# DRAM scratch of the split queries and keys with a gap behind every two heads, and each store issued in two

## What is computed

```python
h = tok(x)                 # embedding (8000 x 128) + positions, 4 layers: 8-head attention, norm, 512-wide ReLU MLP, norm
h = h + nystrom(norm(h))   # landmark attention with a pseudo-inverse and a convolution
h = h + moe(norm(h))       # frequency transform, 8 experts, 2 taken
h = h + wide(norm(h))      # 8 heads of width 128
h = h + routed(norm(h))    # a router picks, per sequence, one of three attentions of 8 heads of width 16
```

## Time and profile before

| | |
|---|---|
| three runs | 1120.76, 1120.85, 1116.46 us; median 1120.76 |
| profiled execution | span 1115.5 us; no time of its own is listed beside the three; the lowest of them is 0.96 us over the span |
| mean TensorE clock granted | 0.925 of full speed |
| busy | TensorE 980.4 us (88%), VectorE 606.8, ScalarE 593.6, GpSimd 425.6 |
| token layers | 0 to about 495 us; touched stores and loads between 22.9 and 406 us |
| blocks without touched code | about 495 to 1004 us |
| last block | touched stores and loads between 1017.6 and 1071 us, end at 1115.5 |
| DMA | 54,416 packets, 71.82 MB |

### The profile page before, as it was taken

One profiled execution on the slowest core, in us unless ns is written; L12 is line 12 of the kernel. 1 busy time (PEld: TensorE's weight loads), 2 busy tenths in 40 slices (PEclk: granted clock), 3 DMA queues, 4 the chain that ended last, 5 costly groups with the idle time before them and its releaser, 6 DMA issues. The chain is left out here.

```text
span 1115.5 us, 21061 instructions
## 1 busy us (share of the span) xinstructions
PE 980.4 (88%) x7350; PEld 707.9 (63%) x7350; DVE 606.8 (54%) x1802; ACT 593.6 (53%) x1332; POOL 425.6 (38%) x620
## 2 busy tenths in 40 slices
PE   2499999999999998635896999996899999997898
PEld 1256666666666665323685667775688888885564
DVE  4366766666667664126354111116277777784773
ACT  4166676676666665316534543325455555543476
POOL 6326777776667666548003000014400000037200
PEclk9689999999999999866698899998799999996899
DMA  4755444645564440010100011010000010006841
GB/s 131 166 106 131 94 93 100 149 111 108 108 143 94 93 96 9 1 33 0 46 3 9 20 30 38 19 34 1 20 11 11 11 54 15 1 1 146 205 96 37
DMA packets 54416, 71.82 MB, mean 64 GB/s; under 512 B 9476, under 2 KB 46624, under 8 KB 50464
## 3 DMA queue, kind: packets, MB, share of 16 engines
q1 hardware_dynamic: 53160, 67.33, 26.0%
q0 software_dynamic: 1152, 3.15, 1.2%
HBM read 48.96 MB, written 17.56 MB: 60 GB/s over the span
## 5 line engine op out<-in xcount | busy, mean ns | idle before, releaser
L2231 DVE TENSOR_REDUCE t_nmax<-banks 128x2 f32<-128x512 f32 x256 | 166.6, 685 | 90.9 <-PE banks L2041 83.7
L2160 ACT ACTIVATE t_probs<-banks 128x512 f32<-128x512 f32 x256 | 144.9, 592 | 80.1 <-PE banks L2063 79.0
L2041 PE MATMUL banks<-t_packed 96*128 96x256 bf16 x512 | 91.3, 279 | 15.3 <-DMA t_packed<-t_qk_pairs 12.8
L2319 POOL TENSOR_SCALAR xhat<-t_rbuf,mv,rstd 128x128 f32<-128x128 f32 x128 | 100.1, 795 | 3.4
L2063 PE MATMUL banks<-t_packed 120*128 120x256 bf16 x512 | 92.6, 278 | 9.1 <-DMA t_packed<-t_mT 8.6
L2041 PEld LDWEIGHTS banks<-t_packed 96*128 96x128 bf16 x512 | 46.7, 99 | 57.7 <-issue 27.2
L858 ACT ACTIVATE hid<-banks,b 128x512 f32<-128x512 f32 x64 | 43.5, 686 | 69.0 <-PE banks L763 68.3
L2063 PEld LDWEIGHTS banks<-t_packed 120*128 120x128 bf16 x512 | 46.4, 99 | 48.2 <-issue 21.2
L1192 ACT ACTIVATE l_probs<-banks,l_shift 128x256 f32<-128x256 f32 x128 | 59.4, 472 | 28.2 <-DVE l_shift L1233 25.5
L2076 PE MATMUL banks<-t_probs,t_v 128*32 128x256 f32 x1024 | 72.9, 389 | 0.5 <-ACT t_probs L2160 0.5
L901 DVE SCALAR_TENSOR_TENSOR acc<-banks,gates,acc 128x128 f32<-128x128 f32 (+1 forms) x72 | 20.1, 342 | 97.8 <-PE banks L783 97.8
(11 more groups left out here) (374 smaller groups left out, 2091.1 us busy)
## 6 DMA issues: line engine op xcount, KB each, us to landing
t_qk_pairs<-t_parts SPq DMA_DIRECT2D x32, 384.0 KB, 2.5
t_packed<-t_qk_pairs SPq DMA_DIRECT2D x32, 384.0 KB, 5.3
t_packed<-t_qk_pairs SPq DMA_DIRECT2D x32, 256.0 KB, 5.9
t_packed<-t_qk_pairs SPq DMA_DIRECT2D x32, 128.0 KB, 6.7
w<-in_L_ffn_w SPq DMA_DIRECT2D x16, 256.0 KB, 2.7
t_packed<-t_mT SPq DMA_DIRECT2D x32, 96.0 KB
g_qk_pairs<-g_parts SPq DMA_DIRECT2D x8, 384.0 KB, 5.1
g_packed<-g_qk_pairs SPq DMA_DIRECT2D x8, 384.0 KB, 5.0
```

The lines of the kernel that those rows point to most:

```text
L2041: ins = pe.matmul(m.mbank[:, n % 3, i * S:(i + 1) * S], m.packed[0:MROW, 0, p, h, c + qt * P:c + (qt + 1) * P], m.packed[0:MROW, 1, p, h, ...
L2160: act.activation(m.probs[:, n % 6, :], m.sbank[:, n % 2, :], ACT.Exp).then_inc(sem["probs_ready"], 1)
L2231: dve.tensor_reduce(m.nmax[:, b, u // 4, 2 * hp:2 * hp + 2], m.mbank[:, n % 3, :].rearrange("p (i k) -> p i k", i=2), AX.X, ALU.max, negat ...
L2319: ins = pool.tensor_scalar(m.xhat[:, k, i, :], m.rbuf[:, k, i, :], m.mv[:, k, i, 0:1], m.rstd[:, k, i:i + 1], ALU.subtract, ALU.mult)
```

## The change

The scratch gets rows of two heads (2 KB) with 256 unused elements (512 bytes) behind each, so that the 8 KB of one d are now four pieces of 2 KB, 2.5 KB apart. A load's three DMAs read 4 pieces of 2 KB per partition. The partitions of `parts` that belong to even and odd heads go into different halves of a scratch row, and each has a DMA of its own: a store is two DMAs, over the even and over the odd partitions (64 partitions, 192 pieces of 1 KB each). The waits on stores count 32 where they counted 16. Nothing else changes: number of loads, bytes, the order of the steps.

```diff
+ROW_HEADS, ROW_GAP = 2, 256
...
-    scratch = nc.dram_tensor(prefix + "qk_pairs", [2, PAIRS, 3, P, PW], BF16)
+    scratch = nc.dram_tensor(prefix + "qk_pairs", [2, PAIRS, 3, P // ROW_HEADS, ROW_HEADS * PW + ROW_GAP], BF16)
...
-            sp.dma_start(scratch[k, g].rearrange("a p n -> p a n"), parts[:, k, g % 2]).then_inc(stored[k][g % 2], 16)
+            for j in range(ROW_HEADS):
+                sp.dma_start(scratch[k, g, :, :, j * PW:(j + 1) * PW].rearrange("a q n -> q a n"), parts[j:P:ROW_HEADS, k, g % 2]
+                             ).then_inc(stored[k][g % 2], 16)
...
-            sp.wait_ge(stored[k][g % 2], 16 * (g // 2 + 1))
+            sp.wait_ge(stored[k][g % 2], 16 * ROW_HEADS * (g // 2 + 1))
...
-                sp.dma_start(packed[row * DK:(row + count) * DK, k, g % G_SLOTS],
-                             scratch[k, g, part:part + count].rearrange("a (d h) n -> (a d) h n", h=H)
+                sp.dma_start(packed[row * DK:(row + count) * DK, k, g % G_SLOTS].rearrange("p (i j) n -> p i (j n)", j=ROW_HEADS),
+                             scratch[k, g, part:part + count, :, 0:ROW_HEADS * PW].rearrange("a (d i) n -> (a d) i n", d=DK)
...
-                act.wait_ge(stored[k][g % 2], 16 * (g // 2))
+                act.wait_ge(stored[k][g % 2], 16 * ROW_HEADS * (g // 2))
```

More of the change, by code:

```diff
@@ L1957, in store @@
             sp.wait_ge(sem["split_done"], 2 * g + k + 1)
-            sp.dma_start(m.scratch[k, g % PAIRS].rearrange("a p n -> p a n"), m.parts[:, k, g % 2]).then_inc(sem["keys_stored"] if k else sem["parts_stored"], 16)
+            for j in range(ROW_HEADS):
+                sp.dma_start(m.scratch[k, g % PAIRS, :, :, j * PW:(j + 1) * PW].rearrange("a q n -> q a n"), m.parts[j:P:ROW_HEADS, k, g % 2]
+                             ).then_inc(sem["keys_stored"] if k else sem["parts_stored"], 16)
         def load(k, g):
-            sp.wait_ge(sem["keys_stored"] if k else sem["parts_stored"], 16 * (g + 1))
+            sp.wait_ge(sem["keys_stored"] if k else sem["parts_stored"], 16 * ROW_HEADS * (g + 1))
             for row, part, parts in ((0, 0, 3), (3, 0 if k else 1, 2), (5, 0 if k else 2, 1)):
-                sp.dma_start(m.packed[row * DK:(row + parts) * DK, k, g % PAIRS],
-                             m.scratch[k, g % PAIRS, part:part + parts].rearrange("a (d h) n -> (a d) h n", h=H)
+                sp.dma_start(m.packed[row * DK:(row + parts) * DK, k, g % PAIRS].rearrange("p (i j) n -> p i (j n)", j=ROW_HEADS),
+                             m.scratch[k, g % PAIRS, part:part + parts, :, 0:ROW_HEADS * PW].rearrange("a (d i) n -> (a d) i n", d=DK)
                              ).then_inc(sem["packed"][g % PAIRS], 16)
@@ L2137, in _ @@
                 if g >= 2:
-                    act.wait_ge(sem["keys_stored"] if k else sem["parts_stored"], 16 * (g - 1))
+                    act.wait_ge(sem["keys_stored"] if k else sem["parts_stored"], 16 * ROW_HEADS * (g - 1))
                 act.activation(m.parts[:, k, g % 2, 0 if k else 2], lin[turn[("Ak" if k else "Aq", g)][0]], ACT.Identity,
@@ L2350, in tok_transformer @@
     attention_memory(nc, m, banks, stack, "t_")
-    m.scratch = nc.dram_tensor("t_qk_pairs", [2, PAIRS, 3, P, PW], BF16)
+    m.scratch = nc.dram_tensor("t_qk_pairs", [2, PAIRS, 3, P // ROW_HEADS, ROW_HEADS * PW + ROW_GAP], BF16)
     m.hidden = sb("hidden", [P, 4, PW])
```

## The result

The changed kernel takes 1126.18 us (median of four runs, 1124.26 to 1127.13); four runs of the kernel before on the same chip give 1119.5. The ratio is 1.0067, 95% interval 1.0051 to 1.0084: slower by 6.7 us or 0.67%. The forecast was +2.0 us. The profiled execution has a span of 1124.3 us and a time of its own of 1126.15; the granted TensorE clock is 0.925 in the mean, as before.

What follows compares the result with a forecast made beforehand. TensorE, busy 88%, with transfers mattering only where it waits for them. Start 0.45, second pair 0.45, six waits 0.5 and last block 0.6 sum to 2.0 us, on the median 1120.76 giving 1122.8; range 1112 to 1129.

Steps and rivals of the forecast that it cites:

- the piece cost as hidden (0): In the q and k loads: smaller pieces cost 12.5 ns each per engine, taken as adding 0 to the time.
- The dear bound: In the loads: the piece cost if the engine itself is the limit, 0.45 us a pair.
- The rival in which the loads get faster: At the q and k loads: smaller pieces or the gap raise their rate; in full 1112 us; gain over 0.5%: chance 0.2.
- The second half is issued 0.45 us behind the first: At each store: the second DMA's issue makes the store land about 0.45 us later, bounds 0 and 1.2 us.
- At the second pair: Second pair: q loads start later, so x0 lands later and TensorE waits longer, +0.45 us.
- the third line of the sum: TensorE's six waits for DMAs between 60 and 470 us: at most 2.7 us more, taken as 0.5.
- The last block: Last block: later stores delay its products by 0.45 us and its x waits add 0.15, together 0.6 us.
- The slower rival: At each store, ahead of its loads: halves over alternate partitions run at half rate, 1129 us; chance 0.17 with queue trouble.
- a delay of about 1.1 us per store: At the stores: the delay from which the slower rival's total loss passes 5.6 us.
- a first load 3.5 us or more behind its store: At the start: the sign that would show the slower rival; the forecast expected about 2.9 us.
- No change by over 0.5%: Whole kernel: time stays within 0.5% (5.6 us), the forecast and a small gain together; chance 0.63.
- both dear bounds: Whole sum with 1.2 us per store and 0.45 us a pair for pieces: 7 us.

Runs made afterwards that it cites:

- pieces_only: Kernel before with whole stores and no gap, each load reading four overlapping 2 KB pieces per row; ratio to the kernel before 1.0000.
- gap_one_head: Changed kernel with scratch rows of one head, so a store is one DMA and loads read 1 KB pieces; ratio to the kernel before 0.9995.
- split_only: Kernel before with each store as two DMAs over even and odd partitions, no gap, 8 KB pieces; ratio 1.0086.
- split_k: Kernel before with only the keys' store as two DMAs over even and odd partitions; ratio 1.0072.
- split_q: Kernel before with only the queries' store as two DMAs over even and odd partitions; ratio 1.0024.
- two_small: Kernel before, nothing split, with two unread 4 KB DMAs issued behind each keys' store in the layers; ratio 1.0030.
- split_halves: Kernel before with each store as two DMAs over partitions 0 to 63 and 64 to 127; ratio 1.0119.

## Why the forecast came out as it did

- **What the loads gain.** "I take the loads' rate as unchanged, the piece cost as hidden (0)": right for the time. 188 and 182 GB/s against 195 and 194, and ratios of 1.0000 and 0.9995 for 2 KB and 1 KB pieces. The dear bound, 0.45 us a pair, is not seen in the kernel's time; at the start alone something of it may be: from the first load's issue to the first product, 11.7 us before, pieces_only takes 11.9 and gap_one_head 12.2, in one execution each. The rival in which the loads get faster falls: no cut and no pitch raised the rate, which agrees with the port rule of the Trainium skill that the prediction drew on. Its rule on large row pitches, which the prediction also weighed ("DMA: Bandwidth & Descriptors", section "Latency and other measured facts"), is for pitches far above these, and a gap changed nothing that can be seen here (gap_one_head, and the change against split_pieces).
- **What a second DMA costs.** "The second half is issued 0.45 us behind the first": too low. I took a load's issue time for a half store's, and a half store takes 0.61 us, and the first half has become as dear as the second. The first load went from 2.44 to 3.06 us behind the first store, +0.62 where 0.45 was said; at the first product +0.66 (gap_one_head, with whole stores, shows +0.48 there). At the second pair TensorE waits 5.23 us for x0 against 4.40, where +0.45 was said, but this wait tells nothing of the stores: it is 4.37 in split_only, with both stores in two, and 5.23 in pieces_only, with none.
- **The step that failed** is the third line of the sum: "The six waits of 60 to 470 us ... at most 6 x 0.45 = 2.7. ... I take 0.5." It had two faults. The delay of the q loads is not that of one store's landing but sk's issue, 2 x 0.61 - 0.37 = 0.85 us, because sk stands directly ahead of lq; I had passed over it with "in the start waits for landing anyway", which holds for the first pair and not for the steady ones (split_k 1.0072, split_q 1.0024). And the line counted the waits that exist. Where x0 arrived just in time there was no wait to count, and eight more appeared: 12 for 4. By the trace of before, the distance from lq to x0 and x0's landing would have shown how near the other pairs were. Measured: +4.2 us over the twelve steady pair-steps instead of 0.5. Of split_k's +5.2 there, issue time alone gives +2.8 (two_small); the rest stays open.
- **The last block**: 0.6 forecast, +2.76 in the profile, with TensorE's wait there 5.7 us against 2.9. Two kernels without a split store show +2.0 and +2.4 in this stretch, and one with every store in two (split_halves) -0.2, so the profiles do not tell 0.6 from 2.8 or from nothing; this term is not shown either way.
- **The slower rival** had the right place and direction, a store that is dearer than one issue; the bound to pass was "a delay of about 1.1 us per store". Its reason, half rate over alternate partitions, is not what was found: the even and odd halves land in 2.3 us, sooner than the whole store, and what was to show it, a first load 3.5 us or more behind its store, did not come (3.06). The halves that do share ports (split_halves) are the ones that land later.
- **No change by over 0.5%** had 0.63, and the result is 0.17% past that bound, on the side that had 0.17; 1126.18 is inside the range, between the forecast's 1122.8 and the rival's 1129. That the sum with both dear bounds, 7 us, is so near the measured 6.7 is luck: it is made of 1.2 us a store and 0.45 us a pair for the pieces, and neither was found.

## What to carry to other kernels

Before cutting a DMA in two, read its issue time for the new shape and see what stands directly behind it on the same queue: in front of a wait a second issue cost nothing in the steady pairs (split_q), and in front of loads that something small is queued behind it delayed them by its full length (split_k). A delay is to be priced on all places where an arrival is just in time, not on the waits that the trace already shows. And where pieces are of 1 KB and more into the same partitions, cutting them otherwise is not worth an edit here, for better or worse.

## What was not expected of the hardware

- A DMA over 64 partitions takes longer to issue than one over 128 with the same pieces: 0.61 us against 0.37, contiguous or every second partition. The loads go from 0.42 to 0.60 us when a piece of 8 KB is four of 2 KB with a gap, and 0.61 with eight of 1 KB; four overlapping pieces take 0.47 (pieces_only). The reasons are open.
- Pieces of 1 KB, 81,296 packets in place of 54,416, cost nothing that can be seen in the time (0.9995, 0.9975 to 1.0015).
- The same 96 KB transfers on another engine's queue, beside loads in 8 KB pieces that now come six in a row, made the kernel 6.8% slower, and TensorE's waits for them grew from 4.2 to 44.5 us. The Trainium skill, "DMA: Bandwidth & Descriptors", section "Queues, rings and completion order", has each DMA engine take turns between its queues, a packet at a time, a packet there being a run of typically 9 to 17 descriptors and not one of the pieces counted here. No run here shows the turns themselves, nor parts them from the six loads in a row; the waits (44.5 us, and 23.8 with the smaller pieces) would fit them.
